# Decoder layer with a routed feed-forward part: the last steps of the expert blocks in another order

## The reference

```
x = x + attention(norm(x))        # 16 heads, 4-bit weights with scales
x = x + cross_attention(norm(x), ctx)
x = x + moe(norm(x))
```

```
h = silu(x W1[e]) * (x W3[e])        # 256 -> 176
y[token] += weight[token, e] * (h W2[e])   # 176 -> 256, for the 4 experts e of the token
```

## Time and profile before

| what | value |
|---|---|
| timed runs | 537.72, 539.82, 540.89 us; median 539.82 us |
| span of the profiled execution (first to last instruction) | 548.9 us |
| mean granted clock of TensorE in it | 0.982 |
| PE busy | 505.7 us (92%) |
| DVE busy | 401.6 us (73%) |
| device memory read / written | 57.79 MB / 28.48 MB |

### The profile page before, as it was taken

The page is one execution under the profiler, slowest core; times in us unless marked ns, Lnnn a source line. Parts: engine busy times, 40 slices in busy tenths (PEclk is TensorE's granted clock), DMA queues, the critical chain, the costliest instruction groups (busy, mean ns, idle before and its releaser), DMA issues.

```text
span 548.9 us, 12557 instructions
## 1 busy us (share of the span) xinstructions
PE 505.7 (92%) x4841; PEld 412.0 (75%) x4841; DVE 401.6 (73%) x968; ACT 252.9 (46%) x560; POOL 199.0 (36%) x172
## 2 busy tenths in 40 slices
PE   6988999999999999999999999899837899999984
PEld 5777888888878888566667666677737788989883
DVE  6699875636645477899599677998745799657766
ACT  2454656636485463001121332763314598665552
POOL 7856450003100000433455232217556334544440
PEclk8899999999999999999999999999988999999999
DMA  8235100025071059992000003502541773456543
GB/s 293 105 158 196 44 2 1 2 97 201 4 239 60 2 183 355 323 325 80 1 1 2 2 1 119 192 2 78 203 134 67 235 255 104 135 168 187 158 129 116
DMA packets 22299, 68.09 MB, mean 124 GB/s; under 512 B 3979, under 2 KB 12595, under 8 KB 21204
## 3 DMA queue, kind: packets, MB, share of 16 engines
q1 hardware_dynamic: 17180, 54.45, 30.0%
q0 software_dynamic: 3600, 8.43, 4.2%
q10 hardware_dynamic: 1460, 4.40, 2.2%
HBM read 57.79 MB, written 28.48 MB: 157 GB/s over the span
## 4 chain that ended last, share of the span: by engine, by line
PE 67%; DVE 21%; issue 6%; ACT 2%; POOL 1%; another core or an unknown queue 1%; DMA 1%; ACTq 0%; POOLq 0%; DVEq 0%
PE psum L619 11%; PE psum L776 9%; PE psum L699 6%; PE psum L632 5%; PE psum L970 5%; PE psum L790 4%; PE psum L684 4%; DVE EW L1588 3%; DVE tt L1401 3%; PE psum L652 2%; PE psum L661 2%; PE psum L761 2%; PE psum L843 1%; PE psum L880 1%; PE psum L852 1%
## 5 line engine op out<-in xcount | busy, mean ns | idle before, releaser
L1754 POOL TENSOR_TENSOR rp<-tt,tt 128x512 f32<-128x512 f32 x24 | 30.9, 1288 | 134.4 <-DVE tt L1401 134.4
L1401 DVE TENSOR_TENSOR tt<-psum,tab 128x512 f32<-128x512 f32 x96 | 60.1, 680 | 11.7 <-PE psum L776 10.7
L970 PE MATMUL psum<-EW,xgh 128*128 (+1 forms) x188 | 56.4, 342 | 2.0 <-DVE xgl L1617 1.9
L1795 POOL DMA_INDIRECT parts_of_tokens<-yb,xg x35 | 35.4, 1010 | 54.1 <-issue 32.1
L619 PE MATMUL psum<-xTh,W 128*128 128x512 f32 x128 | 52.4, 410 | 1.7 <-DVE W L1299 1.7
L619 PE MATMUL psum<-xTl,W 128*128 128x512 f32 x128 | 51.4, 401 | 0.0
L1363 DVE TENSOR_TENSOR OTl<-psum,OTh 128x256 fp32r<-128x256 f32 (+1 forms) x49 | 23.2, 502 | 26.7 <-ACT OTh L1084 26.7
L776 PE MATMUL psum<-xTh,Ah 128*128 128x512 f32 x96 | 40.1, 418 | 0.0
L1787 POOL DMA_INDIRECT rows_of_experts<-xe,posi x32 | 32.8, 1024 | 19.1 <-issue 8.6
L776 PE MATMUL psum<-xTh,Al 128*128 128x512 f32 x96 | 38.0, 396 | 0.0
L776 PE MATMUL psum<-xTl,Ah 128*128 128x512 f32 x96 | 38.0, 396 | 0.0
(11 more groups left out here) (263 smaller groups left out, 1453.0 us busy)
## 6 DMA issues: line engine op xcount, KB each, us to landing
rows_of_experts<-in_empty SPq DMA_DIRECT2D x8, 2064.0 KB, 25.6
exr<-in_ex SPq DMA_DIRECT2D x9, 608.0 KB, 7.8
xg<-rows_of_experts SPq DMA_DIRECT2D x39, 129.0 KB
exr<-in_ex ACTq DMA_DIRECT2D x7, 608.0 KB, 5.6
yv<-parts_of_tokens SPq DMA_DIRECT2D x8, 512.0 KB, 4.6
raw<-in_codes SPq DMA_DIRECT2D x6, 512.0 KB, 6.5
raw<-in_codes SPq DMA_DIRECT2D x3, 1024.0 KB, 8.0
wor<-in_woc SPq DMA_DIRECT2D x4, 512.0 KB, 3.8
```

The lines of the kernel that those rows point to most:

```text
L970: mm = pe.matmul(ap[:, 0:352], xp[b % 2][:, 128 * kt:128 * kt + 128], piece(b, o + 352 * kt, 352), start=(k == 0), stop=(k == 5))
L1401: return tt_(b3(tt[n][:, :], 64), b3(src, 64), tab[:, j % 3, n, :].unsqueeze(1).to_broadcast([128, 8, 64]), ALU.mult)
L1754: tt_(o[:, 0, :], tt[0][:, :], tt[1][:, :], ALU.subtract).then_inc(s_rp_lo, 1)
L1795: nc.gpsimd.indirect_dma_start(out=parts_of, out_offset=to, in_=yb[b % 4][:, :], in_offset=None, bounds_check=4 * 1024 - 1, oob_is_err=Fal ...
```

## The change

Only the order of entries in the last steps changes, and one count with it. No instruction is added or removed.

```diff
@@ block_order @@
-    for s in range(MIDDLE_TO, NB + 2):
+    for s in range(MIDDLE_TO, NB - 1):
...
-        if s >= NB - DIRECT + 3:
-            step += [("direct", s - (NB - DIRECT + 3))]
...
-        if s == NB + 1:
-            step += [("direct", DIRECT - 1)]
-        for t in range(NT - 1):
-            if s == min(BLOCKS_OF[t] + 3, NB + 1):
+        for t in range(NT - 2):
+            if s == BLOCKS_OF[t] + 3:
                 step += [("results", t)]
...
-        if s == NB - 1:
-            step += [("results", 7)]
-        for k in range(DIRECT):
+        for k in range(2):
             if s == NB - DIRECT + k + 1:
                 step += [("match", k)]
         yield step
-    yield [("add_direct",)] + [("total", 6, k) for k in range(3)] + [("total", 7, k) for k in range(3)]
+    yield [("results", 6), ("results", 7), ("store", 4, 2)]
+    yield [("block_hidden", NB - 1), ("block_back", NB - 2), ("block_down", NB - 3), ("block_back", NB - 1)]
+    yield [("direct", 0), ("match", 2), ("block_down", NB - 2), ("direct", 1), ("match", 3), ("block_down", NB - 1)]
+    yield [("direct", 2), ("direct", 3), ("total", 5, 2)]
+    yield [("total", 6, k) for k in range(3)] + [("add_direct",)] + [("total", 7, k) for k in range(3)]
     yield [("store", 6, 1), ("store", 7, 1)]
@@ total @@
-                y4, n = yv[t % 4], 2 * t + (t >= 6)
+                y4, n = yv[t % 4], 2 * t + (t == 7)
```

## The result

Over 22 runs each the median went from 539.61 us to 537.52 us; the ratio of the runs is 0.9963, 95% interval 0.9945 to 0.9981, a gain of 2.0 us (1.0 to 3.0). The forecast was 538.0 us and a gain of 1.8 us from a median of 539.82. A second measurement of the same kernel (8 runs against 31) gave 0.9930 (0.9904 to 0.9957), a gain of 3.8 us: two such comparisons can differ by nearly as much as the whole effect, and the traces have to tell what it is made of.

The account below looks back on a forecast made before the run. DVE's seven closing sums bound the end: beginning when load 6 lands (541.7), plus 3.45 us, plus 1.9 us for the last store, they gain 1.8 us. So 539.82 - 1.8 = 538.0 us, range 538.0 - 1.6 to 540.3.

Parts of the forecast that it names:

- best case: Load 6 starts at 537.05 and takes 4.1 us, so DVE's own order binds at 541.2; gain 2.3 us.
- Part 1: On PE, block 46's turn back moves ahead of products 0 and 1; its transposes start 1.13 us earlier.
- part 2: On PE, products go between projections; product 3 ends at 542.3 instead of 543.43, gaining 1.15 us.
- Part 3: On DVE, `total 5,2` moves behind match 3, tile 6's sums ahead of `add_direct`; seven sums could begin 2.3 us earlier.
- Part 4: On SP, loads 6 and 7 go ahead of store 4; load 6 starts at 537.5 and lands at 541.7.
- the last store's row: At the kernel's end, bytes flow until 548.40, span ends 548.9; read as up to 0.5 us from last byte to signal.
- block 38's pair: Block 38's scatter began at 525.18, the load waiting for it at 529.17: 3.99 us, the only measured pair.
- the rule of the Trainium skill: For DMA, most of a fixed 2 us lies between last byte and semaphore; block 42's signal would come about 539.05.
- A: Block 42's scatter signals late, at 539.1, so load 6 holds DVE until 543.3; gain 0.2 us, 539.6; chance 0.15.
- B: Late load 6 holds all seven DVE sums, since tile 6's precede `add_direct`; 0.6 us slower, 540.4; chance 0.05.
- C: PE's clock halves at 539, products ready only at 545.3; gain nil or 0.2 us lost, 539.9; chance 0.05.
- D: Load 7 meets store 4 and load 6 and lands late, delaying tile 7's sums; gain 1.2 us, 538.6; chance 0.13.

Follow-up runs that it names:

- e3: Kernel before with loads 6 and 7 ahead of store 4 on SP and tile 6's sums ahead of `add_direct` on DVE, PE unchanged; ratio 0.9971.
- e6: Changed kernel with store 4 put back ahead of loads 6 and 7 on SP; ratio to the kernel before 1.0061.
- e7: Changed kernel with part of tile 7's closing sums moved from DVE to PE as products with the identity; ratio to the kernel before 0.9980.
- e1: Kernel before with only loads 6 and 7 moved ahead of store 4 on SP; ratio 1.0016.
- e2: Kernel before with only PE's and DVE's new order, `total 5,2` kept early, SP and order of the seven sums unchanged; ratio 1.0022.
- e4: Kernel before with loads 6 and 7 first and PE's new order, `add_direct` still first of the seven sums, `total 5,2` early; ratio 0.9969.

## Why the prediction was right

**What bounds.** Right. DVE's seven sums end the kernel, 3.45 us predicted and 3.48 measured, and the end is their beginning plus a constant. The last store took 535.5 - 533.60 = 1.9 us, as predicted. Of the conditions, load 6 came last in the second trace (DVE waited 0.4 us for it); in the first it landed within 0.02 us of the end of DVE's own work, so there the forecast and its best case fall together.

**Part 1 and part 2, the products.** The order of steps was right, the sum 0.35 us too long: transposes of block 46 at +2.95 (predicted +2.93), projection 45 at +3.54 (+3.73), projection 46 at +4.57 (+4.9), product 3's end at +6.8 (+7.2). The leg gained 1.5 us instead of 1.15; I had taken 0.51 us from a product's start to the start of what follows it, from product 1 and the transposes behind it. In the new order a projection follows, and projection 45 starts 0.32 behind product 0 (527.20 to 527.52). The rows of before had that pair: product 2 at 540.82, the projection behind it at 541.14, 0.32. Since DVE did not wait for the products any more, this error did not reach the forecast.

**Part 3, the sums.** Right, and more important than it looked: e3 shows that the order of the sums alone is worth 1.5 us once the loads are early. `total 5,2` ended at +6.0 (+6.1 predicted).

**Part 4, the loads.** The term with the widest bounds, 537.05 to 538.99, came out at the value taken: 537.5 is +2.38, measured +2.35 and +2.36. What gave it was the quiet stretch of the DMA row with the last store's row as the distance from bytes to signal; block 38's pair, 3.99 us, would have been wrong by 1.6 us. Part of this is luck. The store's row was read the wrong way round: bytes that end by 548.40 and a span that ends at 548.9 make at least 0.5 us, not at most; the 0.45 that I took behind 537.05 held because the distance is about that. And a store of 128 KB stood for a scatter that, as the packets show, wrote nothing; the rows gave no reason why the two should agree, nor did the prediction see that block 42 writes no row. How late the signal of a scatter of real rows comes stays open. Nor did the store's row speak against the rule of the Trainium skill: that section is on transfers that GpSimd starts, and SP starts the store. The time to land was taken as 4.2, with 4.1 as the shortest, and was 3.70 in one trace and 3.99 in the other, both below that bound. That is the term that was mis-sized, by 0.2 to 0.5 us, and it makes most of the difference between the predicted yardstick (13.8 - 1.8 = 12.0) and the measured 11.5 and 11.8. Load 7 missed on the other side: 5.3 and 5.5 us, where 5.0 was taken as the longest.

**The rivals.** A: no, by the windows above. B did not occur here, but e6 shows its mechanism at full size: with load 6 at +10.9 all seven sums stand behind it and the kernel is 0.6% slower. C: no, the granted clock (the column before the last two) was 1.00 until the last product had ended at 530.78, and product 3 takes the same 0.67 us as before:

```profile
528.00:529.40 1.40, 1.40 (x12) 1.29 (x11) 1.22 (x8) 0.47 (x1) 0.00 (x0) 1.00 0.94 372
529.40:531.00 1.60, 1.16 (x5) 0.38 (x3) 1.45 (x4) 0.47 (x1) 0.00 (x0) 1.00 0.77 298
```

In the trace of before the clock fell earlier than rival C says: the window 546.0 to 546.5 has a mean of 0.81 and all behind it 0.50. PE had no work left by then. D: near. e7's wait puts load 7's landing at +8.1. In the changed kernel it takes 5.3 us and lands at about +8.0, just when tile 7's first sum starts (532.00, +8.0, right behind `add_direct`). It cost nothing visible, but there is no slack left.

**The size.** That 537.52 us lies so near 538.0 owes something to the base: the median of three runs that differ by 3.2 us happened to be within 0.2 us of that of 22. The chance of 0.82 for no measurable change stood on the best case of 2.3 us, 0.43%. The traces show 2.0 to 2.3, the runs 0.19% to 0.55%, the second measurement 0.43% to 0.96%. Neither interval holds "no change": 22 runs each tell 0.2% apart here, not only the 0.5% that the prediction went by.

## What to carry to other kernels

When an engine waits at the end for one of two things, moving one of them alone may bring nothing: here the early loads gained nothing (e1) and the early products nothing or worse (e2), and both together 1.5 us (e4). Look for work on the waiting engine that depends on the other input only, and put it into the wait (e3): that gave the same 1.5 us without touching the slow leg. Shortening that leg on top of it gave the last 0.4 to 0.7 us (12.2 against 11.5 and 11.8). And when work is delayed to make room, look for a queue that stands still for its result; the same reordering costs 0.6% with the store in front of the loads and gains 0.4% with it behind.

For measuring: two executions of identical instructions differed by 11 us ahead of the changed part. A tail of 12 us can be compared only from a common event at its beginning, and even then two traces of one kernel differ: by less than 0.1 us for the kernel before, by 0.3 for the changed one, by 0.5 for e2.

## What was not expected of the hardware

- The start of the scatter to the load that waits for it took 2.34 to 2.36 us in each kernel with the loads first (e1: 527.94 - 525.60; after: 526.33 - 523.98), with nothing else in the DMA queues and no row to write; the like pair for block 38 took 3.99 us among other transfers. Whether the traffic or the rows make the difference was not tested.
- Two loads of 512 KB each started at the same distance from the same scatter, behind the same store, were slow in both traces of e2 (load 6 landed after 4.7 and 6.1 us) and not in the two of before (4.1 and 3.9). What decides it is open.
- A 128x256 product of float32 is two instructions on PE; two such products with nothing between them start 0.53 us apart (e7: 532.05 and 532.58).
